# Attention scores from a two-way float32r split of q and k in place of a three-way bf16 split

## The reference

```python
q = (src @ q_w).reshape(b, s, h, hd).transpose(0, 2, 1, 3)      # b=2, s=2048, h=16, hd=16
k = (src @ k_w).reshape(b, s, h, hd).transpose(0, 2, 1, 3)
v = (src @ v_w).reshape(b, s, h, hd).transpose(0, 2, 1, 3)
scores = jnp.einsum('bhqd,bhkd->bhqk', q, k) / np.float32(np.sqrt(hd))
scale = jax.nn.sigmoid(jnp.einsum('bhsd,hd->bhs', q, scale_w)) * 2.0
aw = jax.nn.softmax(scores * scale[..., None], axis=-1)
out = jnp.einsum('bhqk,bhkd->bhqd', aw, v).transpose(0, 2, 1, 3).reshape(b, s, d)
```

## Time and profile before

| | |
|---|---|
| runs (us) | 2486.89, 2488.21, 2483.85; median 2486.89 |
| profiled execution, first to last instruction | 2487.7 us |
| TensorE busy / VectorE / ScalarE / GpSimd | 2369.6 / 2102.9 / 1796.4 / 992.7 us |
| granted TensorE clock, mean | 0.976 of full speed |
| attention with its lead and tail | about 720 to 2140 us of the span |

### The profile page before, as it was taken

The page is one execution under the profiler, slowest core; times in us unless marked ns, Lnnn a source line. Parts: engine busy times, 40 slices in busy tenths (PEclk is TensorE's granted clock), DMA queues, the critical chain, the costliest instruction groups (busy, mean ns, idle before and its releaser), DMA issues. The chain is left out here.

```text
span 2487.7 us, 45337 instructions
## 1 busy us (share of the span) xinstructions
PE 2369.6 (95%) x16331; PEld 1028.3 (41%) x16331; DVE 2102.9 (85%) x4156; ACT 1796.4 (72%) x2368; POOL 992.7 (40%) x1186
## 2 busy tenths in 40 slices
PE   7899999999689999999999999999999999996996
PEld 5566655655443223223222222223223222473663
DVE  6778788989689999999998999898899996283886
ACT  4888887777334887878787787787787878762664
POOL 1687878888741222211221221221211011255664
PEclk8999999999889999999999999999999999997998
DMA  3322233223240220304012030040040000125892
GB/s 110 112 88 90 85 92 105 89 99 96 67 137 14 37 43 7 59 14 65 14 31 35 14 59 7 14 65 2 14 65 2 2 2 24 52 83 204 297 304 101
DMA packets 105956, 174.09 MB, mean 70 GB/s; under 512 B 21218, under 2 KB 80658, under 8 KB 100596
## 3 DMA queue, kind: packets, MB, share of 16 engines
q1 hardware_dynamic: 98996, 156.08, 23.6%
q0 software_dynamic: 6016, 14.49, 1.7%
q10 hardware_dynamic: 720, 0.62, 0.1%
HBM read 145.21 MB, written 27.02 MB: 69 GB/s over the span
## 5 line engine op out<-in xcount | busy, mean ns | idle before, releaser
L1682 DVE TENSOR_REDUCE max_part<-round_psum 128x1 f32<-128x512 f32 x2048 | 1269.0, 683 | 101.8 <-PE round_psum L1591 96.8
L1647 ACT ACTIVATE p_exp<-score_psum 128x1024 f32<-128x1024 f32 x1024 | 993.3, 1022 | 213.7 <-PE score_psum L1576 209.3
L1591 PE MATMUL round_psum<-k_stack,q_stack 64*128 64x512 bf16 x2048 | 705.5, 384 | 10.7 <-DVE max_part L1682 6.5
L1567 PE MATMUL score_psum<-q_stack,k_stack 64*128 64x512 bf16 x2048 | 599.0, 379 | 0.9 <-ACT p_exp L1647 0.2
L1576 PE MATMUL score_psum<-q_stack,k_stack 35*128 35x512 bf16 x2048 | 594.6, 378 | 0.0
L1622 PE MATMUL pv_psum<-p_exp,values 128*17 128x512 f32 x4096 | 539.6, 598 | 0.0
L1591 PEld LDWEIGHTS round_psum<-k_stack,q_stack 64*128 64x128 bf16 x2048 | 189.4, 93 | 600.3 <-DVE max_part L1682 510.7
L672 PE MATMUL rot<-tokens_t,w_in 128*128 128x512 f32 x576 | 271.7, 603 | 0.2
L1576 PEld LDWEIGHTS score_psum<-q_stack,k_stack 35*128 35x128 bf16 x2048 | 188.9, 94 | 116.0 <-issue 0.5
L1729 POOL TENSOR_TENSOR rden<-pv_out,minus_one 128x16 f32<-128x16 f32 x31 | 90.0, 2903 | 332.4 <-ACT pv_out L1665 330.1
L1715 POOL CAST max_parts<-max_neg 128x16 bf16<-128x16 f32 x96 | 20.4, 212 | 365.8 <-DVE max_neg L1688 343.4
(11 more groups left out here) (300 smaller groups left out, 3472.9 us busy)
## 6 DMA issues: line engine op xcount, KB each, us to landing
cum_rows_in<-cum_rows SPq DMA_DIRECT2D x64, 512.0 KB, 3.8
expert_w<-in_expert_w SPq DMA_DIRECT2D x24, 1028.0 KB
tokens_t<-in_expert_w SPq DMA_DIRECT2D x15, 1028.0 KB
cum_pairs_in<-cum_rows SPq DMA_DIRECT2D x240, 64.0 KB, 2.8
qk_rows<-qk_parts SPq DMA_DIRECT2D x64, 192.0 KB, 3.1
q_stack<-qk_rows SPq DMA_DIRECT2D x84, 128.0 KB, 8.1
k_stack<-qk_rows SPq DMA_DIRECT2D x84, 128.0 KB, 9.1
token_rows<-tokens SPq DMA_DIRECT2D x12, 512.0 KB, 3.7
```

Of the source, the lines that this page charges most:

```text
L1567: nc.tensor.matmul(ebank[i // 2][:, i % 2, :], ks[rows, n % 2, plane, k * P:(k + 1) * P], qs[rows, n % 2, plane, q * BLK:(q + 1) * BLK], s ...
L1591: nc.tensor.matmul(bank[step][:, :], qs[rows, n % 2, plane, at:at + P], ks[rows, n % 2, plane, keys * BLK:(keys + 1) * BLK], start=True, s ...
L1647: nc.scalar.activation(pt[:, (k * 2 + pair) % 4, :, :], ebank[pair][:, :, :], ACT.Exp).then_inc(*exped.up(u, k, pair))
L1682: nc.vector.tensor_reduce(mx[:, c * HG + h, keys:keys + 1], bank[step][:, :], AX_X, ALU.max).then_inc(*maxed.up(u, k, i))
```

## The change

q and k are split into two parts: the value rounded to float32r, and what is left of it, exactly. Three products of parts are taken (`Q_TERMS = (0, 0, 1)`, `K_TERMS = (0, 1, 0)`), 48 rows, and two rows subtract the maximum: 50 rows, all in float32r, so that a head and chunk needs one "score" matmul. The max matmuls use 48 rows, in float32r too. The maximum is split into two parts by GpSimd and transposed in float32. The "low" steps of ScalarE and GpSimd go, the DMAs of the stack fall from 24 to 12 for a group with twice the bytes each, and the rows of ones are written by 16 DMAs in place of 4, from a tile that GpSimd fills. The weights and parts of the split now share the place of the gate's weights, so that the gate's loads wait for the last split.

```diff
-Q_TERMS = (0, 0, 1, 1, 0, 2)
-K_TERMS = (0, 1, 0, 1, 2, 0)
+Q_TERMS = (0, 0, 1)
+K_TERMS = (0, 1, 0)
 TERMS = len(Q_TERMS)
-MROWS = 3
+MROWS = 2
...
-        self.qs = sb("q_stack", [P, 2, HG, SEQ], BF16)
-        self.ks = ks
+        self.qs = sb("q_stack", [P, 2, HG // 2, SEQ], F32R)
+        self.ks = sb("k_stack", [P, 2, HG // 2, SEQ], F32R)
...
@@ split_on_scalar
-            nc.scalar.copy(p[:, 0, :], x).then_inc(*S.high.up(n, s))
-    if what == "low":
-        for s, x, p, _ in S.blocks(j):
-            act.wait_ge(*S.rest.at(n, s))
-            nc.scalar.copy(p[:, 1, :], x).then_inc(*S.low.up(n, s))
+            nc.scalar.copy(p[:, 0, :].bitcast(F32R), x).then_inc(*S.high.up(n, s))
@@ attention_order
-        for left, right in ((("max", 0), ("main", 1)),
-                            (("main", 0), ("rest", 1)),
-                            (("rest", 0), ("max", 1)),
-                            (("max", 2), ("main", 3)),
-                            (("main", 2), ("rest", 3)),
-                            (("rest", 2), ("max", 3))):
+        for left, right in ((("max", 0), ("score", 1)),
+                            (("score", 0), ("max", 1)),
+                            (("max", 2), ("score", 3)),
+                            (("score", 2), ("max", 3))):
@@ attention, TensorE
-                if what == "main":
+                if what == "score":
                     n, q = UNITS[u]
-                    rows, plane = main_of(i)
+                    rows, plane = rows_of(i, SCORE_AT)
                     if i % 2 and (u, k) != (0, 0):
                         pe.wait_ge(*exped.at(*back(u, k, 1), i // 2))
...
-                    nc.tensor.matmul(ebank[i // 2][:, i % 2, :], ks[rows, n % 2, plane, k * P:(k + 1) * P],
-                                     qs[rows, n % 2, plane, q * BLK:(q + 1) * BLK], start=True, stop=False)
-                if what == "rest":
-                    n, q = UNITS[u]
-                    rows, plane = rest_of(i)
...
                     m = nc.tensor.matmul(ebank[i // 2][:, i % 2, :], ks[rows, n % 2, plane, k * P:(k + 1) * P],
-                                         qs[rows, n % 2, plane, q * BLK:(q + 1) * BLK], start=False, stop=True)
+                                         qs[rows, n % 2, plane, q * BLK:(q + 1) * BLK], start=True, stop=True)
...
-                    turned = bank[step][0:HG * MROWS, 0:BLK // 2].bitcast(BF16)
+                    turned = bank[step][0:HG * MROWS, :]
...
-                                                K["identb"])
+                                                K["ident"])
@@ attention, GpSimd
-                    for part in range(MROWS):
-                        if part:
-                            po.wait_ge(*pool_own.last())
-                        nc.gpsimd.tensor_copy(mparts[:, :, part], neg[:, :]).then_inc(*part_of.up(u, part))
...
+                    nc.gpsimd.tensor_copy(mparts[:, :, 0].bitcast(F32R), neg[:, :]).then_inc(*part_of.up(u, 0))
+                    po.wait_ge(*part_of.at(u, 0))
+                    nc.gpsimd.tensor_tensor(mparts[:, :, 1], neg[:, :], mparts[:, :, 0],
+                                            ALU.subtract).then_inc(*part_of.up(u, 1))
```

More of the change, by code:

```diff
@@ L10 @@
 BF16 = mybir.dt.bfloat16
+F32R = mybir.dt.float32r
 U32 = mybir.dt.uint32
@@ L1051, in __init__ @@
         self.scale_loaded = sems.dma("w_sc_load", [0])
-        self.filled = sems.dma("rows_fill", [(slot, odd) for slot in range(2) for odd in range(2)])
+        self.fills = list(itertools.product(range(2), range(2), range(HG // 2), range(2)))
+        self.filled = sems.dma("rows_fill", self.fills)
         self.projected = sems.events("qk_projected", blocks)
@@ L1197, in stage3_step @@
     what, at = word.rstrip("0123456789"), [int(i) for i in word.lstrip("abcdefghijklmnopqrstuvwxyz")]
+    if what in ("fill", "ones"):
+        return [(what, 0, 0, 0)]
     if what == "stack":
@@ L1296, in on_scalar @@
                 split_on_scalar(nc, act, S, b, j, what, i, bank[what, b, j, i])
-            if what in ("high", "low"):
+            if what == "high":
                 split_on_scalar(nc, act, S, b, j, what, i, None)
@@ L1362, in on_gpsimd @@
             c = slice(b * CPB, (b + 1) * CPB)
+            if what == "ones":
+                nc.gpsimd.memset(ones, 1.0).then_inc(*ones_in.up(0))
             if what == "mixed":
@@ L1544, in _ @@
                     stack_on_sync(nc, sp_, S, u, j, i, scored.at((u - 1) * SB - 1, KT - 1, 1) if u >= 2 else None)
-            sp_.wait_ge(*scored.at(NU - SB - 1, KT - 1, 1))
+            sp_.wait_ge(*S.rest.at(len(GROUPS) - 1, SB - 1))
+            for save in S.saved:
+                sp_.wait_ge(*save.all())
             for name in GATE_LOADS:
@@ L1641, in _ @@
                 what, u, k, i = step
-                if what == "rest" and i % 2 == 0:
+                if what == "score" and i % 2 == 0:
                     pair = i // 2
@@ L1777, with __init__, take @@
 BUSY5 = {"gate0": 2, "place1": 2, "place3": 14, "logits5": 2, "rows6": 4, "place5": 2, "logits6": 1}
+class SplitPlace:
+    def __init__(self, place):
+        at = [0]
+        def take(*shape):
+            first, at[0] = at[0], at[0] + math.prod(shape)
+            return place[:, first:at[0]]
+        self.w_qk = take(KD, NG, 3 * HG * HD).rearrange("p (k g c) -> p k g c", k=KD, g=NG)
+        self.parts = take(2, 2, BLK).rearrange("p (i part c) -> p i part c", i=2, part=2)
+        self.ez = take(BLK)
 class GateInputs:
@@ L2646, in layout @@
     o["v_w"] = kt(a["v_w"])
-    o["ones_rows"] = np.full((MROWS, SEQ // 2), 0x3F803F80, np.uint32).view(np.float32)
     q = a["q_w"].reshape(KD, P, NG, HG * HD)
```

103 lines of the change are left out of this document (44 added, 59 removed).

## The result

The changed kernel takes **2605.07 us** (2604.04 to 2606.42, 4 runs) against 2485.37 (2483.14 to 2488.21, 4 runs) for the kernel before: ratio **1.0476, 95% interval 1.0462 to 1.0490**. The profiled execution has a span of 2604.6 us, 116.9 more than before.

A forecast was written before the change was run, and what follows sets the result against it. A 2.48 us chain through VectorE's maxima, max matmuls and weigh was taken as the bound, not TensorE's load. Loads 45, transposes 7, lead 1, tail -3, rest -1 gave +49 on 2487.7: 2536 us, range 2480 to 2605.

The forecast's parts named there:

- the circle: Each step's chain: VectorE's first maximum, fourth max matmul, weigh, next first max matmul, its maximum; 2.48 us, no score matmul.
- The weight load: Two uncovered float32r loads per step, at the fourth and next first max matmul, 57 ns against 11: +45 us.
- rival 1: An uncovered float32r load of the max matmuls costs what a float32 one does, 105 ns: 2584 us; chance 0.20.
- Score matmuls: Two of six score slots go, 0.44 us a step; outside the chain that sets the step, so gain 0.
- Speed of a float32r matmul: A float32r matmul of 512 columns takes one stream, 376 ns once its weights are in, so no cost.
- turn_rows: Four transposes between weigh and the next max matmul become float32, 53 ns more each, 32 times: +7 us.
- The rows of maxima by DMA: Still four DMA issues, 2.69 us, landing before the first score that needs them; nothing counted.
- Tail: In the 20 last steps fewer score matmuls can take away ScalarE's wait of 0.27 us per two steps: -3 us.
- GpSimd and ScalarE: GpSimd's shorter chain before the transposes was not waited for; ScalarE's earlier exponentials are outside the circle: no gain.
- The lead: The 16 or so early steps that wait the same way as later ones: +1 us.
- Rival 3: TensorE's load is the bound after all, so steps fall to VectorE's 2.39 us: 2448 us; chance 0.09.

The follow-up runs named there:

- e7: The changed kernel with matmuls of zeros added in the lead alone, where TensorE waits: 2600.39 us, ratio 1.0466.
- e1: The changed kernel with max matmuls reading the upper 16 bits of q and k as bf16, scores still float32r: 2510.44 us, ratio 1.009.
- e15: The changed kernel with the transposes of the maxima in bf16, from upper halves, in place of float32: 2600.16 us, ratio 1.0457.

## Why the prediction was wrong

The forecast was 2536, and the result 2605, just above the range of 2480 to 2605. The direction, the circle and its members held; one term was mis-sized, and one was missing.

**The weight load: the step that failed.** "I take 57" for an uncovered float32r load, between the bounds 11 and 105. After a wait the matmul was to last 433 ns and lasts 491 to 501: 105 to 115 more than the bf16 one's 386, where I had 46 and rival 1 had 94 (in the circle: 0.31 to 0.42 ahead of weigh, 0.39 to 0.50 behind it). I had chosen by the number of streams, as if a load took as long as its matmul's passes; the transposes, which I took as the nearest row, were not near. It is rival 1, to which I gave 0.20, and its sign came too: the load takes 183 ns, where my forecast wanted about 140 and rival 1 190. The term measures 98 us between the weighs (89.7 by the bf16 maxima, and the 0.02 in 367 steps, 8, by which that run's matmuls were themselves slower) in place of 45; rival 1's own term was 92. The section "Weight-path perf modes — Fast Weight Load (FWL) and DoubleRow" of the Trainium skill's "TensorE: Matmul & The Clock Gate" keeps the fast load to types that are not FP32. The 183 ns here, against 93 in bf16, show that float32r has no fast load either. I had that rule, and the estimate of 94 us beside it, and weighed the transposes' 57 ns heavier. That estimate came from the section "LDWEIGHTS (loading the stationary operand)" of the same page of the Trainium skill, whose columns / 1.2 make 107 ns of a load of 128 columns; the trace has 183 for the load itself, and 105 to 115 for what it adds uncovered. With the bounds that far apart and each worth 92 us, 0.42 against 0.20 was too sure.

**Score matmuls: right.** Worth nothing in a plain step, shown by both sides: taking four of eight away before gives 5 us in all and leaves the step at 2.475; giving the others a short load after gives none. VectorE's idle time before its maxima grew by 119 us for the 50 that I named, since the step grew by 0.22 and not by 0.09.

**Speed of a float32r matmul: right.** One stream: from 387 ns where its load is covered, for the 376 that I took.

**turn_rows: right in place, short in size.** +7 was the streams. Measured 9 in 26 steps (0.34 each without the loads of the max matmul), since the float32 transposes also start 0.11 later behind weigh.

**The rows of maxima by DMA: right**, no wait for them in a plain or a turn_rows step shows. **Tail:** -1.2 for -3. **GpSimd and ScalarE: right**, no term.

**The lead: missing.** +1 was predicted for it, and it is +14.6. My sum took each row's duration at full clock into the changed kernel, and TensorE is at half its clock for about 47 of the 75 us there (the five stretches above), for about 15 of 60 before (my expectation for e7 had 54 and 18).

Together, between the profiled spans: 98 for the loads and 9 for turn_rows, 3.4 less in tail and single steps, 14.6 in the lead, -2.4 before it and +1.1 after the last weigh: 116.9.

**Rival 3 was rightly low.** The fourth max matmul starts 0.75 us after the first maximum (1985.97 to 1986.72), just as before: VectorE, not the scores, lets it go.

## What to carry to other kernels

Follow the chain that returns to itself through the engines and count only what stands in it: here two weight loads of 0.11 us were worth 100 us, and a third of the 512-column matmuls next to nothing. A buffer that is awaited has a holder; a move opens such a circle only if it changes which instruction holds it, and three banks tie the matmul behind weigh to the one ahead of the next weigh in any order. A move can also close another circle: here, weigh in the middle of the step had to wait for its own exponentials. And float32r saves streams, not loads: here a float32r matmul whose load can't be covered took 105 to 115 ns more than a bf16 one.

## What the runs showed of the hardware

- A float32r load of 128 columns takes 183 ns on 48 or 50 rows, float32 on 128 rows 190, and bf16 93. The float32r matmul of 512 columns is one stream, 387 ns at the shortest.
- Less work for TensorE can slow a kernel: with weigh at one bf16 stream the granted clock of the changed kernel fell to 0.60 and its time rose by 80 us, with two streams it was 0.99; the kernel before kept 1.00 with one.
- An uncovered 512-column matmul took 397 ns on bf16 views of every second element (e1) and 386 on plain bf16 tiles (before); rows and neighbours differed too, so the view is not shown to be the reason.
- A bf16 transpose starts 0.87 us after weigh (before and e15), a float32 one or a max matmul of either type 0.98 to 0.99; why is not shown.
